# Latent attention: order of the last pair of heads, and its last work placed in attention step 0

## What is computed

```
q_hk = (hidden_q @ Wq.T).reshape(b, s, H, K)
q_big = einsum('bshk,hkq->bshq', q_hk, w_kc_q)
kv_rope = kv_c * cos + rotate_half(kv_c) * sin
q_r = einsum('bshq,hqr->bhsr', q_big, W_qr)
k_r = einsum('bld,hdr->bhlr', kv_rope, W_kr)
attn = softmax(einsum('bhsr,bhlr->bhsl', q_r, k_r))
ctx_c = einsum('bhsl,bld->bhsd', attn, kv_rope)
out = einsum('bhsd,hkd->bshk', ctx_c, w_kc_kv) @ Wo.T
```

## Time and profile before

| what | us |
|---|---|
| median of 3 runs | 996.13 |
| the runs | 991.34, 996.13, 996.32 |
| the profiled execution's own time | 991.64 |
| its span | 989.8 |
| mean granted clock of TensorE, share of full | 0.996 |
| PE busy | 949.2 (96%) |
| DVE / ACT / POOL busy | 526.4 / 412.8 / 452.6 |

### The profile page before, as it was taken

How to read it: one execution, slowest core, us unless ns; L and a number is a source line. 1 busy time by engine, 2 the same in 40 slices (tenths; PEclk the granted TensorE clock), 3 DMA queues, 4 the chain that set the end, 5 groups by cost and what they waited for, 6 DMA issues and landing times. The chain is left out here.

```text
span 989.8 us, 15941 instructions
## 1 busy us (share of the span) xinstructions
PE 949.2 (96%) x5497; PEld 801.8 (81%) x5497; DVE 526.4 (53%) x976; ACT 412.8 (42%) x956; POOL 452.6 (46%) x489
## 2 busy tenths in 40 slices
PE   6999977999999989999999999999999999999998
PEld 5777756888887867888888988777779999999997
DVE  5434458777888835445454222427786333333345
ACT  2434458787887724333322044463441122222111
POOL 2899856555676621000000402217715878993051
PEclk9999989999999999999999999999999999999999
DMA  8688713111111105222320014402043657571153
GB/s 252 203 265 260 228 54 92 42 39 43 37 39 34 54 1 192 85 85 85 101 90 22 11 43 140 121 14 97 2 147 137 215 188 235 190 231 57 44 160 107
DMA packets 79004, 109.92 MB, mean 111 GB/s; under 512 B 14225, under 2 KB 46993, under 8 KB 78929
## 3 DMA queue, kind: packets, MB, share of 16 engines
q1 hardware_dynamic: 66288, 82.18, 27.0%
q10 hardware_dynamic: 10080, 18.35, 5.2%
q0 software_dynamic: 2560, 8.39, 2.7%
HBM read 83.13 MB, written 25.77 MB: 110 GB/s over the span
## 5 line engine op out<-in xcount | busy, mean ns | idle before, releaser
L43 PE MATMUL psum<-second_xT_hi,second_w_hi 128*128 128x512 f32 x272 | 106.9, 393 | 4.9 <-PEq L74 2.9
L44 PE MATMUL psum<-second_xT_lo,second_w_hi 128*128 128x512 f32 x272 | 106.0, 390 | 0.0
L45 PE MATMUL psum<-second_xT_hi,second_w_lo 128*128 128x512 f32 x272 | 106.0, 390 | 0.0
L1283 POOL TENSOR_TENSOR all_x<-all_x,mlp_raw 128x512 f32<-128x512 f32 x8 | 10.0, 1294 | 173.1 <-DVE all_x L1786 173.1
L2325 ACT ACTIVATE moe_s<-psum 128x352 f32<-128x352 f32 x39 | 18.1, 465 | 149.0 <-PE psum L45 149.0
L43 PEld LDWEIGHTS psum<-second_xT_hi,second_w_hi 128*128 128x128 f32 x272 | 51.0, 188 | 17.6 <-issue 3.7
L1741 ACT ACTIVATE mlp_s<-psum,mlp_side 128x512 f32<-128x512 f32 x32 | 21.9, 683 | 100.3 <-PE psum L45 100.3
L43 PE MATMUL psum<-moe_w_hi,moe_tT_hi 128*128 (+1 forms) x187 | 62.6, 335 | 0.0
L1786 DVE TENSOR_TENSOR all_x<-all_x,psum 128x512 f32<-128x512 f32 x64 | 43.8, 687 | 31.7 <-PE psum L45 31.3
L45 PE MATMUL psum<-moe_w_hi,moe_tT_lo 128*128 (+1 forms) x187 | 60.3, 322 | 0.0
L44 PE MATMUL psum<-moe_w_lo,moe_tT_hi 128*128 (+1 forms) x187 | 60.1, 321 | 0.0
(11 more groups left out here) (347 smaller groups left out, 2849.1 us busy)
## 6 DMA issues: line engine op xcount, KB each, us to landing
kv_all<-all_x ACTq DMA_DIRECT2D x28, 256.0 KB
far_raw<-in_eg SPq DMA_DIRECT2D x10, 704.0 KB, 4.2
far_raw<-in_eu SPq DMA_DIRECT2D x10, 704.0 KB, 4.7
slot_rows<-mix_W SPq DMA_DIRECT2D x23, 256.0 KB, 5.9
slot_out<-far_rows ACTq DMA_DIRECT2D x23, 256.0 KB, 2.5
far_raw<-in_ed SPq DMA_DIRECT2D x10, 512.0 KB, 4.3
far_rows<-slot_rows ACTq DMA_DIRECT2D x19, 256.0 KB, 2.9
second_raw<-in_w_feat SPq DMA_DIRECT2D x18, 256.0 KB, 3.4
```

The lines of the kernel that those rows point to most:

```text
L43: e.matmul(out, hi_l, hi_r, start=first, stop=False)
L44: e.matmul(out, hi_l, lo_r, start=False, stop=False)
L45: return e.matmul(out, lo_l, hi_r, start=False, stop=last)
L1283: pool.tensor_tensor(g["x"][:, t, :], g["x"][:, t, :], b2, ALU.add).then_inc(x_plus, 1)
```

## The change

Three things are altered, in all five lists at once where they meet.

1. In the last pair (p = 7) half 1 is taken before half 0: features(7,1), features(7,0), turn 28, queries(7,1), fold_g(14), turn 29, queries(7,0). A helper `turn_at` gives the count that a semaphore has reached for a half in this order. Turn 29 stands two places later than before.
2. Batches 0 and 1 no longer wait for all 16 query copies but for 15 (`NEEDED`), on both engines.
3. Turn 30, fold_g(15) and turn 31 with ACT's and DVE's share of them go into attention step 0: on PE behind scores(0), on ACT behind exponentials(0, 1), on DVE behind normalise(0, 1). DVE's copy of queries(7,0) and its first_queries(1) stand in step 0 between the maxima and normalise(0, 0). ACT's wait for all turns moves from before step 0 to the end of its moved work, and a wait for all DVE query copies stands beside it.

No arithmetic instruction and no DMA is added or removed.

```diff
+        def turn_at(p, half):
+            return 2 * p + (half if p + 1 < NP else 1 - half)
+        NEEDED = 2 * NP - 1
...
             def queries(p, half):
                 pe.wait_ge(k_kept, p + 1)
-                pe.wait_ge(r_kept, 2 * p + half + 1)
+                pe.wait_ge(r_kept, turn_at(p, half) + 1)
                 for u in range(2):
-                    wait(pe, q_kept[u], 2 * p + half)
+                    wait(pe, q_kept[u], turn_at(p, half))
...
+            p = NP - 1
+            features(p, 1)
+            features(p, 0)
+            turn_context(BPP * p)
+            queries(p, 1)
+            fold_g(2 * p)
+            turn_context(BPP * p + 1)
+            queries(p, 0)
+
+            def last_work():
+                turn_context(BPP * p + 2)
+                fold_g(2 * p + 1)
+                turn_context(BPP * p + 3)
+            made.tensor_last = last_work
...
             def first_queries(s):
-                act.wait_ge(q_kept[0], H)
-                act.wait_ge(q_kept[1], H)
+                act.wait_ge(q_kept[0], NEEDED)
+                act.wait_ge(q_kept[1], NEEDED)
...
+            p = NP - 1
+            keep_features(p, 1)
+            keep_features(p, 0)
+            first_columns(0)
+            keep_queries(p, 1)
+            first_queries(0)
+            first_columns(1)
+            keep_g(2 * p)
+            keep_queries(p, 0)
+            first_queries(1)
+
+            def last_work():
+                context_columns(BPP * p + 2)
+                keep_g(2 * p + 1)
+                context_columns(BPP * p + 3)
+                act.wait_ge(kvT_ok, B)
+                act.wait_ge(q_kept[1], 2 * NP)
+            made.scalar_last = last_work
...
+            p = NP - 1
+            split_features(p, 1)
+            split_features(p, 0)
+            first_columns(0)
+            keep_queries(p, 1)
+            first_queries(0)
+            first_columns(1)
+            split_g(2 * p)
+
+            def last_queries():
+                keep_queries(p, 0)
+                first_queries(1)
+
+            def last_work():
+                split_g(2 * p + 1)
+            made.vector_queries, made.vector_last = last_queries, last_work
...
                 if s < B:
                     scores(s)
+                if s == 0:
+                    heads.tensor_last()
...
-            act.wait_ge(heads.kvT_ok, B)
...
                 if s < B:
                     exponentials(s, 1)
+                if s == 0:
+                    heads.scalar_last()
...
                     maxima(s, 0)
                     maxima(s, 1)
+                if s == 0:
+                    heads.vector_queries()
...
                 if s < B:
                     normalise(s, 1)
+                if s == 0:
+                    heads.vector_last()
```

More of the change, by code:

```diff
@@ L543, in tensor @@
             fold_g(0)
-            for p in range(NP):
+            for p in range(NP - 1):
                 if p > 0:
                     features(p, 0)
[L547 to L550, removed]
+                    fold_n(p + 1)
+                turn_context(BPP * p)
                 features(p, 1)
-                if p + 1 == NP:
-                    turn_context(BPP * p)
                 turn_context(BPP * p + 1)
-                if p + 1 < NP:
-                    fold_a(p + 1)
+                fold_a(p + 1)
                 if p > 0:
@@ L572, in keep_features @@
             def keep_features(p, half):
-                act.wait_ge(r_ready, 2 * p + half + 1)
+                act.wait_ge(r_ready, turn_at(p, half) + 1)
                 act.activation(r_hi[:, half, :], psum[:, RB + half, :], ACT.Copy).then_inc(r_hi_kept, 1)
@@ L594, in first_queries @@
             def first_queries(s):
-                act.wait_ge(q_kept[0], H)
-                act.wait_ge(q_kept[1], H)
+                act.wait_ge(q_kept[0], NEEDED)
+                act.wait_ge(q_kept[1], NEEDED)
                 act.activation(q_hi[:, s, :], q[:, place_of(s), :], ACT.Copy).then_inc(first_q_hi, 1)
             def keep_queries(p, half):
-                act.wait_ge(q_ready, 2 * p + half + 1)
+                act.wait_ge(q_ready, turn_at(p, half) + 1)
                 act.activation(queries_of(2 * p, half), psum[:, XB, :].rearrange("p (g b s) -> p g b s", g=2, s=S), ACT.Copy).then_inc(q_kept[0], 1)
@@ L611, in scalar @@
             keep_g(0)
-            for p in range(NP):
+            for p in range(NP - 1):
                 if p > 0:
                     keep_features(p, 0)
-                if p + 1 < NP:
-                    context_columns(BPP * p)
-                    store_context(BPP * p)
+                context_columns(BPP * p)
+                store_context(BPP * p)
                 keep_features(p, 1)
[L619 to L625, removed]
+                context_columns(BPP * p + 1)
+                store_context(BPP * p + 1)
+                keep_a(p + 1)
                 if p > 0:
@@ L629, in scalar @@
                 context_columns(BPP * p + 2)
-                if p + 1 < NP:
-                    store_context(BPP * p + 2)
+                store_context(BPP * p + 2)
                 keep_queries(p, 1)
-                if p + 1 == NP:
-                    first_queries(0)
                 keep_g(2 * p + 1)
-                if p + 1 == NP:
-                    first_queries(1)
                 context_columns(BPP * p + 3)
-                if p + 1 < NP:
-                    store_context(BPP * p + 3)
+                store_context(BPP * p + 3)
+            p = NP - 1
[15 more added lines that the diff above has]
+            made.scalar_last = last_work
         def vector(v):
@@ L656, in split_features @@
             def split_features(p, half):
-                v.wait_ge(r_hi_kept, 2 * p + half + 1)
+                v.wait_ge(r_hi_kept, turn_at(p, half) + 1)
                 v.tensor_tensor(r_lo[:, half, :], psum[:, RB + half, :], r_hi[:, half, :].bitcast(F32), ALU.subtract).then_inc(r_kept, 1)
@@ L665, in keep_queries @@
             def keep_queries(p, half):
-                v.wait_ge(q_ready, 2 * p + half + 1)
+                v.wait_ge(q_ready, turn_at(p, half) + 1)
                 v.tensor_copy(queries_of(2 * p + 1, half), psum[:, XB + 1, :].rearrange("p (g b s) -> p g b s", g=2, s=S)).then_inc(q_kept[1], 1)
@@ L705, in vector @@
             split_g(0)
-            for p in range(NP):
+            for p in range(NP - 1):
                 if p > 0:
                     split_features(p, 0)
-                    if p + 1 < NP:
-                        keep_n(p + 1)
+                    keep_n(p + 1)
                 split_features(p, 1)
[L712 to L716, removed]
+                split_a(p + 1)
                 if p > 0:
```

## The result

| | before | after |
|---|---|---|
| median of 6 runs each, us | 995.95 | 989.83 |
| lowest and highest | 991.34, 999.57 | 987.60, 990.39 |
| profiled execution, its span | 991.64, 989.8 | 990.39, 988.6 |
| mean granted clock of the profiled execution | 0.996 | 1.000 |

The ratio of after to before is 0.9941, 95% interval 0.9923 to 0.996: 5.9 us faster. Two later comparisons of the same two kernels gave 0.9968 (0.9949 to 0.9988) and 0.996 (0.9938 to 0.9983), which is 3.2 and 4.0 us, so the mean of the three is about 4.4 us, and the first one drew on the lucky side of its interval. Forecast were 991.4 us in 985.3 to 995.3; 991.4 against 996.13 is 0.9952.

The account below looks back on a forecast made before the run. PE, busy 96%, was taken as the bound, with time to win only in its holes at the heads-attention seam. Terms -5.5 + 1.3 - 0.5 gave -4.7 us, from the 996.13 median to 991.4, range 985.3 to 995.3.

Parts of the forecast that it names:

- The path to scores(0): Seam from heads to attention: scores(0) starts at 132.35, 5.3 us earlier, and step 0's first exponential 5.5 us earlier.
- The moved work: Step 0: turns 30 and 31 and fold_g(15) cost PE nothing, but ACT's copies give back 1.3 of 5.5 us.
- rival C: First step: ACT, DVE and PE wait for each other in a ring; gain only 0.5 to 2.5 us; chance 0.05.
- POOL and DVE: After step 0's exponentials: scores(2) comes 4.8 us earlier, and these two engines catching up takes 0.5 us off the gain.
- The multiply: DVE's normalise(1,0) beside POOL: taken as 1.1 us, bounds 0.69 alone and 1.52 as measured before.
- The sum: Whole seam: -5.5 + 1.3 - 0.5 = -4.7 us, bounds -4.0 and -5.3.
- Rival A: Seam: the clock never falls, so the gain is 5.3 to 6.5 us, about 990.2; chance 0.15.
- The fall that A and the sum left open: 1.2 GHz stretch near step 2: up to 0.5 us more won if absent, up to 0.3 lost if it returns.
- B: New step 0: the clock falls inside it, slowing the score blocks; gain 2.6 to 3.8 us, about 993.0; chance 0.20.
- D: Steps 0 to 5: PE stays at 1.2 GHz and the kernel gets slower, about 997.1 us; chance 0.04.
- E: Seam: nothing moves, as another wait holds scores(0) or step 4's context load; about 996.1 us; chance 0.04.
- The signs: New trace: no PE hole over 0.4 us before scores(0), exponentials and scores(2) at named times, span near 985.

Follow-up runs that it names:

- e9: Changed kernel with the last pair's halves in the old order, profiled only; step 2's first exponential 23.50 us after that pair's first features matmul.
- e6: Kernel before with idle transposes filling the 1.62 us hole ahead of turn 29 and the holes of step 1; ratio 0.9972.
- a2: Changed kernel, unchanged, profiled a second time; first exponential of step 5 at 38.55 us from the last pair's first features matmul.
- b2: Kernel before, unchanged, profiled a second time; first exponential of step 5 at 42.72 us from the last pair's first features matmul.
- e2: Changed kernel with halves in the old order and turn 29 in its old place, so only the last work is moved into step 0; ratio 1.0004.
- e8: Changed kernel with turn 29 back directly behind turn 28, profiled only; step 2's first exponential 23.13 us after the last pair's first features matmul.
- e1: Changed kernel with the moved work put back ahead of the attention, halves still swapped and turn 29 late; ratio 0.998.
- e3: Kernel before with only turn 29 moved, behind queries(7,0) and fold_g(14); ratio 0.9975.
- e5: Kernel before with 14 idle transposes in the 1.62 us hole ahead of turn 29; ratio 1.0001.
- e4: Changed kernel with its moved work spread over steps 0 to 2 instead of all in step 0; ratio 0.9958.

## Why the prediction was right

**The path to scores(0)** was forecast at 132.35, which is F+9.69, and came at 9.71. Each piece of it was a start-to-start time of the old trace, and the new trace repeats them; e9's two times, forecast 8.3 and 12.0, came at 8.27 and 11.97 in the same way.

**The moved work** was to give back 1.3 us, and gave 1.16 (5.34 less 4.18). Its cover on PE held, and the new 1.53 us wait ahead of turn 31 is where it was expected (136.5 on the old clock is F+13.84; it came at F+14.01). The ring of waits of rival C costs no more than the hand-overs used.

**POOL and DVE.** scores(2) gained 4.85 for 4.8. The multiply that I put at 1.1 us, between 0.69 and 1.52, took 0.69, but the operation ahead of it took the wait. DVE and POOL in the profile after:

```profile
143.27 1.18 DVE L1061 SCALAR_TENSOR_TENSOR att_scale<-att_last,att_total 128x2 f32<-128x2 f32 x1 [0.64 <-ACT att_last L1008]
144.48 0.17 DVE L1063 RECIPROCAL att_scale<-att_scale 128x2 f32<-128x2 f32 x1
144.68 0.69 DVE L1067 TENSOR_TENSOR queries_q<-queries_q,att_scale 128x512 f32<-128x512 f32 x1
```

```profile
143.16 1.26 POOL L879 TENSOR_TENSOR first_xT_hi<-queries_q,first_xT_hi 128x512 fp32r<-128x512 f32 x1
```

POOL's operation ends at 144.42 and the two-element one on DVE at 144.45: an operation that takes 0.15 alone stood a microsecond for it. The Trainium skill (SBUF — State Buffer, "SBUF: two separate sides") has the shared port pair as an exclusive lock between GpSimd and a VectorE operation with two SBUF inputs. The small operation reads two (att_last and att_total), and the trace agrees. The sum should have put the lock on whichever two-input operation is there, not on the big one. The old trace already showed it: there the small operation stood 0.59 us, until POOL's ended at 144.67.

```profile
144.09 0.59 DVE L1025 SCALAR_TENSOR_TENSOR att_scale<-att_last,att_total 128x2 f32<-128x2 f32 x1 [0.66 <-ACT att_last L973]
143.94 0.73 POOL L841 TENSOR_TENSOR first_xT_hi<-all_x,first_xT_hi 128x256 fp32r<-128x256 f32 x1
```

exp(2,0) gained 4.45 instead of 4.8.

**The clock** is where the forecast was right by luck as well as by reason. I took the first fall as part of the old times and priced the new order at full speed, so 1.5 us of clock were in my 4.7 without a name. Rival A then added the clock a second time: it happened as A says (no fall in the seam, in all three profiles of the change), but the gain was 4.60 and not 5.3 to 6.5. The fall that A and the sum left open, the one at scores(2), was worth 0.15 us in this profile, where up to 0.5 was allowed. e6 gives the split: 2.97 order, 1.63 clock. That the totals came out at the forecast therefore needed a clock that stays up in the new order, and no term of the sum says so. Rivals B and D showed in no profile of the change. E was out with scores(0) at F+9.71.

**Step 5 to the end**: the shift is carried whole in this pair of profiles, 824.07 against 824.08; a2 and b2 have 824.49 and 824.79, each with a fall behind F+242.

**The signs** named ahead came nearly all: exp(0,0) at F+11.53 for F+11.34, scores(2) at F+18.43 for F+18.44, step 4 at F+32.85 for F+32.74. The hole ahead of scores(0) was 0.46 us and not under 0.4. The span was 988.6 and not near 985, because this execution's opening took 3.39 us longer; a2, with F at 122.06, has a span of 985.1.

**The range and the chances.** The chance of more than half a per cent was 0.37, of less 0.60. The three comparisons stand at -0.59, -0.32 and -0.40%, and the seam at 0.46%, so the edge lies inside their scatter, as was said.

## What to carry to other kernels

At a seam between two stages, look for the first piece of work that the new stage needs, and ask what stands ahead of it in each engine's list that it doesn't need: here half a pair of heads, one transpose out of place, and three pieces of last work, each worth 1.5 to 1.9 us only once the others were out of the way too. Work that fills a wait on one engine is not free on the next: what PE did for nothing cost ScalarE 1.2 us, and belongs where ScalarE itself waits. And before a hole is priced from one profile, see at which clock what follows it ran; filling the holes with idle work gave the old order at one clock here, and so the split.

## What the runs showed of the hardware

The clock's fall is not tied to one hole. The kernel before fell behind its 1.62 us hole in one profile of two, and for 3.4 us, and e2 and e8, with the same hole, didn't fall there; a hole of 2.56 us in e2 was followed by a fall, one of 2.73 us in e9 was not. In b2, e1, e3 and e5 the clock fell near scores(2), 17 to 21 us behind F, and for 6.8. What a fall costs depends on where it lies: between exp(2,0) and step 5 the 6.8 us one cost 1.3 us in b2 (18.15 for 16.85 in e6) and 0.65 in e1 (17.50), where it began 3 us earlier; the 3.4 us one inside scores(1) of e4 cost nothing.

The openings differ by about 4 us between executions of one kernel, which goes with totals in two groups: F at 122.66 and 991.64 us in the first profile, F at 127.09 and 996.41 us in b2. In b2 the fold that takes 1.90 us in the first profile (from 17.74) took 3.51, at about half pace, while the windows read a clock of 1.00 there:

```profile
18.14 3.51 PE L479 MATMUL psum<-queries_q,heads_wq 128*128 128x64 f32 x16
```

```profile
15.00:20.00 5.00, 4.35 (x22) 3.84 (x20) 2.77 (x4) 2.33 (x4) 3.02 (x5) 1.00 0.53 152
```

The duration of the matmuls, not the clock column, has to be read so early in a span. Why some openings run so was not tried.
